# Two fp16 parts for the experts' second product, made on Pool, and a scatter split around one chunk's row maxima

## What is computed

```
logits = x @ gate_w.T + gate_b
top_vals, top_idx = top_k(logits, 2)
routing = softmax(top_vals)
for e in range(8):
    h = x @ w1[e].T + b1[e]
    x_glu, x_lin = h[:, 0::2], h[:, 1::2]
    y = x_glu * sigmoid(1.702 * x_glu) * (x_lin + 1.0)
    ye = y @ w2[e].T + b2[e]
    out += ye * sum(routing * (top_idx == e), axis=-1)
```

## Time and profile before

| | us |
|---|---|
| runs | 830.62, 819.61, 827.12 |
| median | 827.12 |
| the profiled execution | 819.61 |
| its span in the trace | 817.8 |

### The profile page before, as it was taken

One profiled execution on the slowest core, in us unless ns is written; L12 is line 12 of the kernel. 1 busy time (PEld: TensorE's weight loads), 2 busy tenths in 40 slices (PEclk: granted clock), 3 DMA queues, 4 the chain that ended last, 5 costly groups with the idle time before them and its releaser, 6 DMA issues.

```text
span 817.8 us, 14289 instructions
## 1 busy us (share of the span) xinstructions
PE 684.2 (84%) x5213; PEld 314.8 (38%) x5214; DVE 599.6 (73%) x1222; ACT 475.7 (58%) x990; POOL 156.5 (19%) x297
## 2 busy tenths in 40 slices
PE   3477879868689999998899989999988998888885
PEld 1244455432223444443444434444434443232432
DVE  5999786599577777777677777777776777788442
ACT  2286767750456655656665666556566656666551
POOL 2322442037600001000100010010001001771112
PEclk9889989885689999999999999999999999999998
DMA  9710325634470352245325523432463321250001
GB/s 293 248 64 0 97 72 165 220 111 147 158 136 2 92 128 84 73 136 144 91 75 118 114 73 91 129 83 72 134 145 74 93 85 43 85 193 21 27 29 49
DMA packets 76850, 85.81 MB, mean 105 GB/s; under 512 B 34170, under 2 KB 60285, under 8 KB 76413
## 3 DMA queue, kind: packets, MB, share of 16 engines
q1 hardware_dynamic: 71114, 74.05, 32.0%
q0 software_dynamic: 3280, 8.98, 3.5%
q10 hardware_dynamic: 2386, 1.87, 0.8%
HBM read 39.54 MB, written 27.53 MB: 82 GB/s over the span
## 4 chain that ended last, share of the span: by engine, by line
PE 55%; ACT 15%; DVE 14%; issue 7%; POOL 5%; ACTq 2%; DMA 1%; SPq 0%; POOLq 0%; DVEq 0%
PE bank L1533 16%; ACT PR L794 8%; PE bank L1469 8%; PE bank L1431 7%; PE bank L1441 5%; PE bank L1492 5%; POOL x_rows L559 4%; PE bank L1303 3%; DVE PM L1195 2%; PE bank L1547 2%; PE bank L1346 2%; ACTq L775 2%; PE bank L1572 2%; ACT U L783 2%; ACT TG L752 1%
## 5 line engine op out<-in xcount | busy, mean ns | idle before, releaser
L794 ACT ACTIVATE PR<-bank 128x512 f32<-128x512 f32 (+3 forms) x640 | 317.2, 537 | 226.0 <-PE bank L1492 124.8
L1195 DVE TENSOR_REDUCE PM<-bank 128x1 f32<-128x512 f32 (+3 forms) x640 | 353.3, 603 | 66.5 <-PE bank L1469 41.4
L1492 PE MATMUL bank<-OPS 57*128 57x512 f16 (+3 forms) x640 | 206.5, 357 | 53.8 <-ACT PR L794 47.6
L1469 PE MATMUL bank<-OPS 54*128 54x512 f16 (+3 forms) x640 | 192.2, 367 | 11.4 <-DVE PM L1195 7.9
L1533 PE MATMUL bank<-PR,VS 128*17 128x512 f32 (+3 forms) x1280 | 156.9, 542 | 0.5 <-ACT PR L794 0.5
L1492 PEld LDWEIGHTS bank<-OPS 57*128 57x128 f16 x640 | 53.3, 93 | 120.4 <-ACT PR L794 110.4
L1469 PEld LDWEIGHTS bank<-OPS 54*128 54x128 f16 x640 | 49.8, 94 | 115.3 <-DVE PM L1195 68.9
L538 POOL TENSOR_TENSOR NP<-NM,NIL 128x8 bf16<-128x8 f32 x32 | 7.7, 240 | 444.4 <-DVE NM L1203 444.3
L1431 PE MATMUL bank<-WB 128*128 128x256 f16 x552 | 80.4, 275 | 0.0
L1431 PEld LDWEIGHTS bank<-WB 128*128 128x128 f16 x552 | 46.1, 98 | 35.9 <-issue 29.4
L1502 PE MATMUL bank<-MASK 64*128 64x64 bf16 x512 | 58.6, 197 | 0.0
(11 more groups left out here) (180 smaller groups left out, 777.3 us busy)
## 6 DMA issues: line engine op xcount, KB each, us to landing
WB<-W SPq DMA_DIRECT2D x23, 512.0 KB, 3.5
OPS<-qk_parts SPq DMA_DIRECT2D x60, 192.0 KB
x_rows<-PR SPq DMA_DIRECT2D x23, 256.0 KB, 3.3
WB<-in_w SPq DMA_DIRECT2D x23, 256.0 KB, 3.4
y_rows<-XT SPq DMA_DIRECT2D x23, 256.0 KB, 3.7
W<-in_w SPq DMA_DIRECT2D x6, 512.0 KB, 6.9
XT<-in_b SPq DMA_DIRECT2D x23, 128.0 KB, 3.7
XO<-in_x SPq DMA_DIRECT2D x4, 512.0 KB, 13.1
```

The costliest lines, as they stand in the source:

```text
L794: act.activation(PR[:, tile % RING, off:CH], PS[2 + tile % 2][:, off:CH], ACT.Exp, scale=1 / SCORE).then_inc(b_exped, 1)
L1195: dve.tensor_reduce(PM[:, c % 2, j, xq, gg:gg + 1], bank[:, 0:width], AX.X, ALU.max).then_inc(a_reduced, 1)
L1469: last = mm(bank[:, 0:width], OPS[ROWS_A, slot, 0, P * (TC * a + xq):P * (TC * a + xq) + P], OPS[ROWS_A, slot, 1, CH * gg:CH * gg + width] ...
L1492: last = mm(bank[:, off:CH], OPS[ROWS_B, slot, 1, P * k:P * k + P], OPS[ROWS_B, slot, 0, CH * b + off:CH * b + CH], start=True, stop=k < T ...
```

## The change

1. `down` takes y and w2 as a high and a low fp16 part each and sums three part products: 12 fp16 matmuls of 256 columns in place of 4 fp32 matmuls.
2. POOL makes the parts. `split_weights(b)`: scale by 16 in place, cast to fp16, subtract, on 512 columns, at step 4 of the block. `split_output(b, f)`: cast and subtract on 256 columns for each half of y, at steps 8 and 17. `down` waits for both. The parts lie in the space of `POSR`, which is no longer read by then.
3. `down` moves from step 18 to step 20 of the block, and with it DVE's `expert_out` and SP's store. In the tables that is 12, 32, 52 and 72 (mod 80).
4. POOL's scatter is cut: after the second chunk's maxima it does tiles 6 to 10, then the third chunk's maxima, then tiles 11 to 15. Before, it did tiles 6 to 15 and then these maxima.
5. Factors of scale move between `gate_linear`, the bias table, `expert_out` and the routing weights, with the same number of instructions.

```diff
-DOWN_AT = {n + 18: b for n, b in BLOCK_AT.items()}
+SPLIT_W_AT = {n + 4: b for n, b in BLOCK_AT.items()}
+SPLIT_Y_AT = {n + 8 + 9 * f: (b, f) for n, b in BLOCK_AT.items() for f in range(2)}
+DOWN_AT = {n + 20: b for n, b in BLOCK_AT.items()}
...
+        W2P = POSB[:, 0, :].rearrange("p (b j f d) -> p b j f d", b=2, j=2, f=KK)
+        YP = POSB[:, 1, :].rearrange("p (b j f n) -> p b j f n", b=2, j=2, f=KK)
...
+            def split_weights(b):
+
+                par = b % 2
+                raw = W2B[par]
+                pool.wait_ge(block_in[par], 80 * (b // 2 + 1))
+                if b >= 2:
+                    pool.wait_ge(ye_ps, b - 1)
+                pool.tensor_scalar(raw, raw, WS, None, ALU.mult).then_inc(w2_scaled, 1)
+                pool.wait_ge(w2_scaled, b + 1)
+                pool.tensor_copy(W2P[:, par, 0], raw).then_inc(w2_high, 1)
+                pool.wait_ge(w2_high, b + 1)
+                pool.tensor_tensor(W2P[:, par, 1], raw, W2P[:, par, 0], ALU.subtract).then_inc(w2_low, 1)
+
+            def split_output(b, f):
+
+                par = b % 2
+                pool.wait_ge(y_ready, 2 * b + f + 1)
+                if b >= 2:
+                    pool.wait_ge(ye_ps, b - 1)
+                pool.tensor_copy(YP[:, par, 0, f], YT[:, par, f, 0:SLOTS]).then_inc(y_high, 1)
+                pool.wait_ge(y_high, 2 * b + f + 1)
+                pool.tensor_tensor(YP[:, par, 1, f], YT[:, par, f, 0:SLOTS], YP[:, par, 0, f], ALU.subtract).then_inc(y_low, 1)
...
             maxima(1)
-            scatter(range(6, NT))
-
-            for n in range(LEAD, STEPS):
+            scatter(range(6, 11))
+            maxima(2)
+            scatter(range(11, NT))
+
+            for n in range(chunk_end(2), STEPS):
                 ended = ends_of(n) if n < TOTAL else None
                 if ended is not None:
                     maxima(ended)
+                if n in SPLIT_W_AT:
+                    split_weights(SPLIT_W_AT[n])
+                if n in SPLIT_Y_AT:
+                    split_output(*SPLIT_Y_AT[n])
...
                 dve.wait_ge(glu_done, 2 * b + f + 1)
+                if b >= 2:
+                    dve.wait_ge(y_low, 2 * b - 3 + f)
...
             def down(b):
 
-                pe.wait_ge(y_ready, 2 * b + 2)
+                pe.wait_ge(w2_low, b + 1)
+                pe.wait_ge(y_low, 2 * b + 2)
+                par = b % 2
                 for q in range(2):
+                    rows = slice(P * q, P * q + P)
                     for f in range(KK):
-                        last = mm(PS[7][:, D * q:D * q + D], YT[:, b % 2, f, P * q:P * q + P], W2B[b % 2][:, f, :],
-                                  start=f == 0, stop=f == KK - 1)
+                        for w, y in ((0, 0), (1, 0), (0, 1)):
+                            last = mm(PS[7][:, D * q:D * q + D], YP[:, par, y, f, rows], W2P[:, par, w, f],
+                                      start=f == 0 and w == 0 and y == 0, stop=f == KK - 1 and y == 1)
                 last.then_inc(ye_ps, 1)
```

More of the change, by code:

```diff
@@ L137, in build @@
         WO1 = sb("WO1", [P, KK, D])
-        POSR = sb("POSR", [ROWS8, 2, S], F16)
+        POSB = sb("POSB", [P, 2, S], F16)
         PICK = sb("PICK", [ROWS8, 2, 4])
@@ L209, in build @@
         TAB = pr32[:, S + D:S + D + E * NT + 8 + 24 + E * E]
+        POSR = POSB[0:ROWS8]
+        W2P = POSB[:, 0, :].rearrange("p (b j f d) -> p b j f d", b=2, j=2, f=KK)
+        YP = POSB[:, 1, :].rearrange("p (b j f n) -> p b j f n", b=2, j=2, f=KK)
         TQ = YT[:, 0]
@@ L300, in build @@
         o_summed = sem("o_summed")
+        w2_scaled, w2_high, w2_low = sem("w2_scaled"), sem("w2_high"), sem("w2_low")
+        y_high, y_low = sem("y_high"), sem("y_low")
         rows_zero, x_scattered, y_added = sem("rows_zero"), sem("x_scattered"), sem("y_added")
@@ L757, in gate_linear @@
                 half = slice(SLOTS * f, SLOTS * f + SLOTS)
-                act.activation(GT[:, b % 2, half], PS[5][:, 0:SLOTS], ACT.Identity,
+                act.activation(GT[:, b % 2, half], PS[5][:, 0:SLOTS], ACT.Identity, scale=1 / 8,
                                bias=BB[:, b % 2, 0, f:f + 1]).then_inc(gate_read, 1)
@@ L1020, in scale_biases @@
             def scale_biases():
-                dve.tensor_scalar(B1S[:, :, 0, :], B1[:, :, 0, :], WS, None, ALU.mult).then_inc(b1_prep, 1)
+                dve.tensor_scalar(B1S[:, :, 0, :], B1[:, :, 0, :], WS / 8, None, ALU.mult).then_inc(b1_prep, 1)
                 dve.tensor_scalar(B1S[:, :, 2, :], B1[:, :, 0, :], 0.851, None, ALU.mult).then_inc(b1_prep, 1)
@@ L1107, in expert_out @@
                 dve.scalar_tensor_tensor(YB[:, b % 2, :].rearrange("p (q d) -> p q d", d=D),
-                                         B2B[:, b % 2:b % 2 + 1, :].broadcast_to([P, 2, D]), 2 * WS ** 2,
+                                         B2B[:, b % 2:b % 2 + 1, :].broadcast_to([P, 2, D]), WS ** 3 / 4,
                                          PS[7][:, :].rearrange("p (q d) -> p q d", d=D), ALU.mult, ALU.add).then_inc(ye_copied, 1)
@@ L1185, in sort @@
                 else:
-                    ins = dve.tensor_scalar(WTS[:, :, :], TOP[:, 1:3, :], 0.5 / WS ** 2, None, ALU.mult)
+                    ins = dve.tensor_scalar(WTS[:, :, :], TOP[:, 1:3, :], 4 / WS ** 3, None, ALU.mult)
                 ins.then_inc(sorting, 1)
```

## The result

The changed kernel takes 820.16 us in the median of 20 runs (814.46 to 825.15), the kernel before 827.87 beside it (819.61 to 833.45). The ratio is 0.9936, with a 95% interval of 0.9912 to 0.9961: 5.3 us less, where 11.6 (1.4%) were forecast. The direction and the range held; by the ratio more than half of the gain did not come, by the medians a third. The profiled execution took 815.30, its span is 813.5.

The account below looks back on a forecast made before the run. No engine was full; PE's chain with ACT's exponentials bound the kernel, `down` nearly always on it. Scatter 7.3 plus loop 4.3 gave 11.6 us, from the median 827.12 to 815.5, range 804 to 824.

Parts of the forecast that it names:

- The scatter: Loop's start: ten DMAs instead of twenty ahead of the third chunk's maxima end PE's 5.74 us wait; gain 7.3 us.
- the upper bound: Start of the loop: 8.8 us gained if all 6.3 us of PE's half-clock stretch after the third turn halve.
- The burst: `down` on PE: twelve fp16 matmuls take 1.33 us in place of 1.93, 0.60 less for each block.
- The move, place by place: `down` two steps later: 1.1 us gained at step 72, 0.15 lost at 12 and 52, 0.1 at 32.
- POOL: POOL's new work: scaling about 0.8 us, 256-column cast 0.41, subtraction 0.65; in time for `down`, and DVE not slowed.
- the sum of the loop, 4.3 us: Gain over all 23 `down` blocks of the loop, of 13.8 us if nothing else moved; period 74.3 us instead of 75.0.
- the scatter brought its 7.3: Rival at the loop's start: another wait takes its place and half of 7.3 us arrives, 819.2 us; chance 0.1.
- "PE bound": Rival for the loop: all 0.60 us arrive at every block, 21.1 us in all with the start, 806.0 us; chance 0.2.
- "DVE held": Rival for the loop: POOL's new work holds DVE, reductions too, 2.3 us a block, 872.8 us; chance 0.05.
- "Late y": Rival at step 72: POOL finishes y's second half late, gain there 0.25 us instead of 1.1, 820.5 us; chance 0.15.

Follow-up runs that it names:

- the split alone: Kernel before with only POOL's scatter divided: ten DMAs, the third chunk's maxima, ten DMAs; 816.37 us, ratio 0.9914.
- the filler: Changed kernel with four useless PE matmuls ahead of the second score of step 19 in each period; 811.10 us, ratio 0.9843 to the kernel before.

## Why the prediction was right or wrong

- **The scatter** (7.3, bounds 5.7 to 8.8): 8.4 in the trace and 7.1 by the runs of the split alone. Right, and the clock behind the turn is full, as the upper bound had it.
- **The burst** (1.33): 1.32. Right.
- **The move, place by place** (a loss of 0.15 at 12 and 52, of 0.1 at 32, a gain of 1.1 at 72): right within 0.05 us by the segments, 52 and 72 taken together. The waits stand where they were forecast and end on what was forecast, 0.97 us at 12 and 52 (forecast 1.1); at step 33 only 0.37 of the forecast 0.8. The turns, moved out of the way, gave back what these steps said the waits cost at 12 and 52; step 32's share was smaller, 0.7 and not 1.2.
- **POOL**: the scaling takes 1.49 where I had 0.8, the subtraction of 256 columns 0.67 (0.65), the cast 0.40 (0.41). In the changed kernel nothing waits for any of it, and DVE isn't held.
- **What failed is the sum of the loop, 4.3 us**, and in it a step that I didn't write down: that the changed loop runs at the clock of the earlier trace rows, 1.00, in every period. It did in one of five. A fall costs 1.2 us, more than the 0.7 that a period gains: the stretch with all `down` measured 0.8 us longer instead of 4.3 shorter, and the product's part is worth nothing in the medians. Where the filler keeps the clock up at that place, the stretch is 3.7 shorter. That the time then came out at 1.57%, even above the forecast 1.4%, may in part be luck: in that profile the tail, with no filler in it, takes 131.8 us against the changed kernel's 134.2.
- The rivals: none of the four was it. The time of "PE bound", 806.0, came only with the turns moved too, the scatter brought its 7.3, and "DVE held" doesn't show in any run. "Late y" doesn't show in the changed kernel; with `down` in its old place it does, at 0.3 us in 12 places.

What stays open is what brings the falls. The new product differs from the old one in its length and in its kind of matmul, and no run parts the two. One period of the changed kernel has no fall though its waits are the same, and the version with two turns moved has none behind its first period. Open too is what decides the falls in the tail, which appear in the profiles of most versions, before's second one among them.

## What to carry to other kernels

Before a saving on PE is summed up, look at what PE does around it: here the clock fell with the shorter burst and stayed up with useless work in a wait, and a fall cost more than the saving, so price a period with and without one. When a burst gets shorter, look for what it used to hide on the other engines: here a copy and two DMA issues on ACT, and moving the turns by two steps was worth more than the change. Before calling an edit useless, compare the stretch that it touches between two traces, and the runs at the same mean clock; and try a few idle matmuls in a wait that PE has anyway.

## What the runs showed of the hardware

- The granted clock fell in a loop where PE is busy 67 of 75 us and its longest wait ahead of the fall, from 312 us on, was 0.97 us; at the same place it stayed up with 1.04 us of matmuls put into a wait of 0.95.
- Time follows a run's mean granted clock closely for one kernel: 574 us per 1.0 over 29 runs of before, with a spread of 1.2 us.
- On POOL a multiplication of 128x512 fp32 by a constant takes 1.49 us, longer than a subtraction of two tensors of that size (1.16 with an fp16 output), and a cast of it to fp16 0.61.
